# Routed feed-forward behind linear attention: which tables count which group, and which slots run after the last step

## The reference

```python
x = x + xattn(layernorm(x), ctx, ctx, ...)   # x, ctx: 128 x 128 x 256, float32
# xattn: q, k, v = linear; elu(q) + 1, elu(k) + 1; 16 heads of 16
#   sums over t of k_t v_t^T, read with q_t (causal), divided by the running sum of q; then @ Wo + bo
x = x + ffn(layernorm(x), W1, b1, W2, b2, expert_W, expert_b)
# ffn: h = relu(z @ W1 + b1); sel = argmax(h @ W2 + b2) over 8 experts
#   out = z @ expert_W[sel] + expert_b[sel], one expert for each token
```

## Time and profile before

| | us |
|---|---|
| median of three runs (range) | 1251.42 (1249.2 to 1252.38) |
| span of the profiled execution, first to last instruction | 1101.6 |
| mean granted TensorE clock in it | 0.977 |
| median less span | 149.8 |

### The profile page before, as it was taken

How to read it: one execution, slowest core, us unless ns; L and a number is a source line. 1 busy time by engine, 2 the same in 40 slices (tenths; PEclk the granted TensorE clock), 3 DMA queues, 4 the chain that set the end, 5 groups by cost and what they waited for, 6 DMA issues and landing times.

```text
span 1101.6 us, 37703 instructions
## 1 busy us (share of the span) xinstructions
PE 1010.6 (92%) x15724; PEld 723.6 (66%) x15724; DVE 879.8 (80%) x1908; ACT 374.5 (34%) x581; POOL 672.5 (61%) x578
## 2 busy tenths in 40 slices
PE   1869999999999999999999999999999999997683
PEld 1446666666777776776677777776676767776472
DVE  2468888998988988888988888888998888885552
ACT  0323333333333343343333333344333333331220
POOL 5134556555666666677666666677766566565755
PEclk9979999999999999999999999999999999998887
DMA  4743434444455445555555544445555544351451
GB/s 139 232 113 101 125 121 125 126 128 145 130 163 160 137 121 145 153 150 164 137 153 163 158 120 126 152 150 163 144 148 165 151 120 128 102 151 41 160 174 53
DMA packets 90920, 152.52 MB, mean 138 GB/s; under 512 B 19325, under 2 KB 57856, under 8 KB 90624
## 3 DMA queue, kind: packets, MB, share of 16 engines
q1 hardware_dynamic: 68864, 107.82, 35.3%
q0 software_dynamic: 12672, 33.84, 8.4%
q10 hardware_dynamic: 9216, 8.46, 3.7%
HBM read 98.20 MB, written 36.13 MB: 122 GB/s over the span
## 4 chain that ended last, share of the span: by engine, by line
PE 78%; DVE 8%; issue 4%; DMA 2%; SPq 1%; POOL 0%; ACT 0%; DVEq 0%; POOLq 0%; ACTq 0%
PE b_a L916 23%; PE b_b L921 18%; PE b_s L1006 9%; PE b_b L953 6%; PE b_s L930 6%; PE b_b L963 5%; DVE stage L634 3%; PE b_s L943 3%; PE b_s L971 2%; PE b_a L911 2%; PE b_s L991 2%; DVE kp L783 1%; DVE st L769 1%; DVE vsel L790 1%; DMA out<-rows 1%
## 5 line engine op out<-in xcount | busy, mean ns | idle before, releaser
L634 DVE TENSOR_TENSOR stage<-b_s,causal 128x1024 f32<-128x1024 f32 x192 | 225.5, 1215 | 6.7 <-PE b_s L930 4.2
L466 POOL DMA_INDIRECT out<-rows x136 | 160.3, 1178 | 45.1 <-issue 34.6
L458 POOL DMA_INDIRECT buckets<-row,place x128 | 141.6, 1106 | 34.5 <-issue 34.2
L916 PE MATMUL b_a<-x_T,wq_sb 128*128 128x512 f32 x256 | 128.9, 628 | 18.7 <-POOL x_T L483 14.2
L475 POOL TENSOR_TENSOR onehots<-onehots,onehot 128x32 bf16<-128x32 bf16 x32 | 7.8, 243 | 193.7 <-DVE place L754 193.7
L921 PE MATMUL b_b<-wo_sb,attT 128*128 128x256 f32 x512 | 121.3, 391 | 2.9 <-DVE attT L831 2.9
L916 PE MATMUL b_a<-ctxT,wk_sb 128*128 128x512 f32 x256 | 118.4, 605 | 1.8 <-ACT pos L530 1.8
L921 PE MATMUL b_b<-wv_sb,ctxT 128*128 128x256 f32 x512 | 119.0, 386 | 0.0
L483 POOL TENSOR_TENSOR x_T<-x_T,scale 128x1024 f32<-128x1024 f32 x32 | 75.5, 2360 | 65.6 <-DMA scale<-scales 64.8
L1006 PE MATMUL b_s<-we_sb,x3T 128*128 x464 | 113.2, 389 | 1.0 <-ACT x3T L539 1.0
L497 POOL TENSOR_TENSOR x_res<-x_res,bias_o 128x1024 f32<-128x1024 f32 x32 | 105.8, 3305 | 5.7 <-DMA x_res<-in_x 5.5
(11 more groups left out here) (125 smaller groups left out, 1794.2 us busy)
## 6 DMA issues: line engine op xcount, KB each, us to landing
rows<-buckets SPq DMA_DIRECT2D x136, 130.0 KB
x_in<-in_x SPq DMA_DIRECT2D x32, 512.0 KB, 4.1
x_T<-in_xT SPq DMA_DIRECT2D x32, 512.0 KB, 4.0
ctxT<-in_ctx SPq DMA_DIRECT2D x32, 512.0 KB, 4.6
qsel<-qp SPq DMA_DIRECT2D x256, 64.0 KB, 2.4
x_res<-in_x SPq DMA_DIRECT2D x32, 512.0 KB
scale<-scales ACTq DMA_DIRECT2D x32, 256.0 KB, 3.9
out<-rows POOLq DMA_INDIRECT x136, 3.4
```

What stands on the lines that cost most here:

```text
L458: pool.indirect_dma_start(buckets, bass.IndirectOffsetOnAxis(place[:, slot(route), t:t + 1], 0), row[:, slot(route), t, :], None).then_inc ...
L466: pool.indirect_dma_start(out.rearrange("t p n -> (t p) n"), bass.IndirectOffsetOnAxis(rows2[:, r, TOKEN:TOKEN + 1].bitcast(U32), 0), rows ...
L634: dve.tensor_tensor(dst.rearrange("p g h s q -> p g (h s) q"), b_s[:, :, 256 * t:256 * t + 256].rearrange("p g (a q) -> p g a q", q=C), ca ...
L916: last = pe.matmul(dst, w[:, k, P * h:P * h + P], rows[:, k, :], start=(k == 0), stop=(k == KC - 1))
```

## The change

- A table is filled in steps 8, 10, ..., 34 (eight slots each), one of four slots in step 35, and the last, now of 20 slots, in step 36. The ranks of the step before a table count the group that is being merged too (four more small products), so the table of step j counts the group routed in step j. SyncE's loads therefore wait for the scatter of that group, which is the one of the step before the loads.
- Quads run in steps 9 to 36. Step 34's quad is an extra one: its turn and products stand between the scores on TensorE, its biases before the second masks on VectorE, its sums after the last masks. Step 35 has two quads: the extra one as before, and one whose turn stands behind that of `x2n` and whose products stand around the logits. The tail has five quads, slots 116 to 135.
- In step 35 GpSimd scatters one tile of the routed group before `scale2` and three after it; before, all four came at the step's end. Extra quads are scattered to `out` in their own step.
- The 20 last slots have their own rows (`tail_rows`, in the memory of the attention's `stage`) and own semaphores, without a wait for the ring. They wait for the attention to be through with `stage`.
- The pads are issued on a signal of their own (`s_pad_at`), ahead of the last table's.
- In the tail no row is loaded ahead of the wait for the buckets.

```diff
-    TABLE_STEPS = range(9, STEPS - 1, 2)
+    TABLE_STEPS = list(range(8, STEPS - 2, 2)) + [STEPS - 2]
+    TABLE_SIZES = [BATCH] * (TABLES - 1) + [QUAD]
+    EARLY = sum(TABLE_SIZES)
+    LAST = SLOTS - EARLY
...
+        tail_rows = stage[:, 0:LAST * ROW].rearrange("p (r n) -> p r n", n=ROW)
...
-        quad_of = quads(TABLE_STEPS[0] + 1, STEPS - 1 - TABLE_STEPS[0], 0)
-        extra_of = {STEPS - 2: quad_of.pop(STEPS - 2)}
-        EARLY = quad_of[STEPS - 1][-1] + 1
+        quad_of = quads(TABLE_STEPS[0] + 1, STEPS - 2 - TABLE_STEPS[0], 0)
+        extra_of = {STEPS - 3: quad_of.pop(STEPS - 3), STEPS - 2: quad_of.pop(STEPS - 2)}
+        quad_of[STEPS - 2] = range(EARLY - 2 * QUAD, EARLY - QUAD)
+        quad_of[STEPS - 1] = range(EARLY - QUAD, EARLY)
...
+        def rows_of(i):
+            return rows2[:, i % RING, :] if i < EARLY else tail_rows[:, i - EARLY, :]
+
+        def rows_in(i):
+            return (s_rows2[i % RING], 16 * (i // RING) + 16) if i < EARLY else (s_tail_rows[i - EARLY], 16)
...
-                    routed = TABLE_STEPS[table] - STAGES
+                    routed = TABLE_STEPS[table] - STAGES + 1
                     sp.wait_ge(s_bucket[routed % 2], 16 * GT * (routed // 2 + 1))
                     sp.wait_ge(s_bucket[1 - routed % 2], 16 * GT * ((routed + 1) // 2))
                     sp.wait_ge(s_tab, TAB * table + TAB)
...
-                    if i >= RING:
-                        sp.wait_ge(s_outs[r], 16 * (i // RING))
+                    if RING <= i < EARLY:
+                        sp.wait_ge(s_outs[i % RING], 16 * (i // RING))
...
-            for quad in TAIL[:1]:
-                load_slots(quad)
             sp.wait_ge(s_spare, 16)
-            sp.wait_ge(s_tab, TAB * TABLES + TAB)
+            sp.wait_ge(s_pad_at, 1)
...
             for e in range(E):
                 sp.dma_start(buckets[bass.ds(pads[e], P), :], pad_row[:, :]).then_inc(s_pad, 16)
+            sp.wait_ge(s_tab, TAB * TABLES + TAB)
+            load_table(mybir.EngineType.SP, TABLES, first_rows)
+            sp.wait_ge(s_o, NG)
             for s in range(2):
                 sp.wait_ge(s_bucket[s], 16 * GT * (NG // 2))
             sp.wait_ge(s_pad, 16 * E)
-            load_table(mybir.EngineType.SP, TABLES, first_rows)
-            for quad in TAIL[1:]:
+            for quad in TAIL:
                 load_slots(quad)
...
+                    if j == STEPS - 2:
+                        scatter_rows(route, range(1))
...
                 if merge and j == STEPS - 2:
                     scale2(merge)
+                    scatter_rows(route, range(1, GT))
...
+                if merge and not attend:
+                    turn_out(slots_of(j))
...
-                turn_out(slots_of(j))
+                if attend or not merge:
+                    turn_out(slots_of(j))
...
+                if attend and extra_slots_of(j):
+                    pe.wait_ge(s_x1, n(merge, 2, 2))
+                    turn(extra_slots_of(j))
                 if attend:
...
                     late_scores(attend, 2, 1).then_inc(s_sb, 1)
+                    multiply(extra_slots_of(j)[0:2])
...
                     early_scores(attend, 1).then_inc(s_sc, 1)
-                if extra_slots_of(j):
+                    multiply(extra_slots_of(j)[2:4])
+                if extra_slots_of(j) and not attend:
...
                     turned(b_a, x2n).then_inc(s_x2Tp, 1)
+                if merge and not attend and slots_of(j):
+                    pe.wait_ge(s_mc, 2 * NG)
+                    turn(slots_of(j))
...
                     logit_products().then_inc(s_lg, 1)
+                if merge and not attend:
+                    multiply(slots_of(j)[2:4])
...
-                    ranks(group_no(merge) == NG - 1).then_inc(s_rank, 1)
+                    ranks(j + 1 in TABLE_STEPS or j + 1 == STEPS - 1).then_inc(s_rank, 1)
```

More of the change, by code:

```diff
@@ L221, in build @@
         s_outs = [sem(f"s_outs{r}") for r in range(RING)]
+        s_tail_rows = [sem(f"s_tail_rows{r}") for r in range(LAST)]
+        s_tail_outs = sem("s_tail_outs")
+        s_pad_at = sem("s_pad_at")
         s_x3Tp = sem("s_x3Tp")
@@ L341, in load_slots @@
             def load_slots(slots):
[L342 removed]
+                if slots and opens_table(slots[0]) and slots[0] < EARLY:
                     table = table_of(slots[0])
[L344 removed]
+                    routed = TABLE_STEPS[table] - STAGES + 1
                     sp.wait_ge(s_bucket[routed % 2], 16 * GT * (routed // 2 + 1))
@@ L454, in scale2, with scatter_rows @@
                                  tokens[:, bass.ds(n(merge, GT), GT)]).then_inc(s_token, 1)
-            def scatter_rows(route):
-                for t in range(GT):
+            def scatter_rows(route, tiles=range(GT)):
+                for t in tiles:
                     pool.indirect_dma_start(
@@ L487, in step @@
                     scale2(merge)
-                if not attend:
-                    for quad in (extra_slots_of(j - 1), slots_of(j - 1)):
-                        scatter(quad)
+                if not attend and j < STEPS - 1:
+                    scatter(extra_slots_of(j))
+                if not attend and j == STEPS - 1:
+                    scatter(slots_of(j - 1))
                 if attend:
@@ L499, in step @@
                                        ALU.add).then_inc(s_xb, 1)
-                if route and j < STEPS - 1:
+                if route and j < STEPS - 2:
                     scatter_rows(route)
+                if attend:
+                    scatter(extra_slots_of(j))
                 if load:
@@ L664, in whole_blocks @@
                 if up:
-                    dve.tensor_tensor(pad_of[:, :], counts, pad_at[:, :], ALU.add)
+                    dve.tensor_tensor(pad_of[:, :], counts, pad_at[:, :], ALU.add).then_inc(s_pad_at, 1)
                 return done
             def fill_table(table, up):
-                first = BATCH * table
-                slots = LAST if up else BATCH
+                first = first_of(table)
+                slots = size_of(table)
                 before_it = TAB * table
@@ L1009, in multiply, with ranks @@
                         last.then_inc(s_prod, 1)
-            def ranks(last_group):
+            def ranks(count_group):
                 out_of = b_a[:, 1, 0:GT * E]
@@ L1110, in step @@
                     expert_means(j - 5)
-                if slots_of(j):
+                if slots_of(j) and (attend or not merge):
                     if not attend:
```

55 lines of the change are left out of this document (29 added, 26 removed).

## The result

| | median us | range, executions |
|---|---|---|
| kernel before | 1250.47 | 1249.2 to 1252.38, 4 |
| changed kernel | 1258.21 | 1256.87 to 1259.4, 4 |

A forecast was written before the change was run, and what follows sets the result against it. TensorE was taken to bound the steps with quads, GpSimd's scatters the tail. Terms -10.4 - 2.4 + 1.4 + 3.4 + 1.3 = -6.7 us gave 1244.7 us from a median of 1251.42; range 1239.5 to 1251.8.

The forecast's parts named there:

- C: Tail's start: eight rows instead of four must land before the first product, 2.2 us lost.
- E: The quad added in step 9: 3.4 us lost, bounds 3.0 to 4.8.
- B: From the last place to the first late row load: pads issued earlier shorten 13.13 us to 8.5, 4.6 us gained.
- F: Counts in the loop: four more small products in the ranks of 14 steps, 1.3 us lost.
- A: Tail: eight scatters fewer at GpSimd's pace of 1.30 us each, 10.4 us gained.
- D, step 34: The quad's turn and products move into TensorE's waits for the masks, 2.0 us gained.
- D, step 35: First quad waits for just-scattered rows and a second quad is added; with step 34's gain, 1.4 us lost in all.
- G: Steps 9 to 33: row loads wait for the step before's scatter, covered by 9.7 us, price 0.
- R5: Rival: row loads, not GpSimd, pace the tail, so the sum comes near 0, 1251 us; chance 0.04.
- R3: Rival: new waits for late landings eat the tail's gain, -1.7 us in all, 1249.7 us; chance 0.16.
- R4: Rival: the loop's new wait makes 13 table-opening quads late; 1 us each gives +6.3 us, 1257.7; chance 0.06.
- signs of being wrong: Loop waits for row loads, gaps among the tail's 20 scatters, or a step 35 much over 16 us.

The follow-up runs named there:

- r0: The kernel before, unchanged, profiled a second time, in the 1250 kind of session: 1247.36 us with a span of 1245.6 us.
- e5: The changed kernel, unchanged, in the 1105 kind of session: 1110.07 us against 1104.61 for the kernel before, ratio 1.0041.
- e2: The kernel before with only the counts changed, so row loads wait for the step before's scatter; 1105 kind: 1104.61 us, ratio 0.9993.
- r1: The changed kernel, unchanged, profiled again in the 1250 kind of session: 1256.38 us.
- e16: The kernel before with own rows for the last 20 slots, pads on their own signal, step 34's quad between the scores; 1250 kind: 1245.3 us against 1249.1.
- e15: The changed kernel with only step 34's quad back in its old place; 1250 kind: 1255.1 us against 1249.1 for the kernel before.
- e3: The changed kernel without the quad of step 9, tail of 24 slots; 1105 kind: 1103.48 us against 1104.83 for the kernel before, ratio 0.9978.
- e6: The changed kernel without step 9's quad and with step 34's in its old place; 1105 kind: 1104.84 us against 1104.61 for the kernel before, ratio 1.0008.
- e9: The same kernel as e16, in the 1105 kind of session: 1102.92 us against 1107.60 for the kernel before, ratio 0.9958.
- e1: The kernel before with only own rows for the last 20 slots and pads on their own signal; 1105 kind: 1101.99 us against 1104.83, ratio 0.9966.
- e14: The kernel before without the scatters to `out` of slots 0 to 95; 1250 kind: 1175.6 us against 1254.22.
- e7: The same kernel as e14, in the 1105 kind of session: 1099.94 us against 1105.32 for the kernel before, ratio 0.9951.

## Why the prediction was wrong

**The step that failed** is the one in the sum: "The median of 1251.42 lies 149.8 us above the span; I leave that part as it is." It was inside the steps. Every price of the loop and of step 34 was then read at the wrong rate: a steady step lasts 36.2 us in r0, 30.9 in the rows. Second, in the kind that the rows did show, C, step 35 and E were too small by 2.9, 2.65 and 2.3 us and the gain of B too large by 1.1. That takes the whole gain away: outside steps 11 to 33 the e5 column adds up to +0.4. The rest of e5's loss lies in steps 11 to 33, where the forecast had 1.3 for F, and stays unexplained. Term by term, us (the tail's split counts from the last ranks; loss positive):

| term | forecast | e5 less before | changed less r0 |
|---|---|---|---|
| A, tail scatters | -10.4 | -10.4 | -12.8 |
| B, to the first late load | -4.6 | -3.5 | -8.4 |
| C, to the first scatter | +2.2 | +5.1 | +10.5 |
| D, step 34 | -2.0 | -2.5 | +4.6 |
| D, step 35 | +3.35 | +6.0 | +2.35 |
| E, steps 8, 9, 10 | +3.4 | +5.7 | +9.3 |
| F, counts | +1.3 | nothing that shows (e2) | not measured alone |
| G, new wait in the loop | 0 | nothing that shows (e2) | not measured alone |
| 11-32 and 33 | 0 | +6.4 | +5.6 (r1: +3.2) |

(D was forecast at +1.35 in all, 2.0 of gain in step 34 included. The last row holds the odd steps as well. The profiled pair differs by 11.2 us and the medians by 7.7, since r0 is a low execution of its kernel.)

**A** was right, by its own reason: 28 scatters in 36.43 us became 20 in 26.00, 1.30 each. In the timed kind they take 1.48 each before and 1.43 after, with gaps of up to 3.1 and 2.1 us. R5 falls for the 1105 kind.

**B** was right in kind. From the last place to the first late load it is 9.1 us in e5 (forecast 8 to 9) in place of 13.1, and 10.5 in place of 17.7 in the timed kind. But what comes last is still the pads: in e5 the landing of the last one, 3.31 us from 1054.87, and in the timed kind SyncE's own issues. Chain of the changed kernel, pads (L422) and row loads (L377):

```profile
1192.65 0.69 SPq L422
...
1202.71 0.71 SPq L377
...
1207.05 0.33 SPq L377
...
1208.08 3.13 DMA stage<-buckets
...
1213.80 6.60 PE b_b L1035 x16
```

**C** was too small. Its sum has one term for TensorE's side, four rows more; in e5, where the loads do follow at 0.54 us, another stands beside it:

```profile
1068.22 5.82 PE L1035 MATMUL b_b<-we_sb,x3T 128*128 x16 [1.81 <-issue]
```

From the first late load to these products it is 9.8 us, 5.0 before (1051.02). The turn of the eighth row ends 8.0 us after that load, where the fourth ended at 5.2: 2.8 us for the four rows more, forecast 2.2. Then TensorE reads the last table, five reads (L311) from 1065.7 to 1068.0, and stands idle for 1.81 us; before, its six reads of the table lay beside the sixteen products. The slow products are no news: 5.82 us, and 5.22 before. In the timed kind SyncE adds to it. Its first late loads are 2.1 to 2.8 us apart while GpSimd issues scatters to `out`, and from 1207.05 on, 1.9 us after the last of these, they are 0.52 apart, so the eighth load stands 8.7 us behind the first, 3.7 in e5. The chain above has both paces. The products take 6.60 us there (granted clock 0.56 over them; 3.72 warm), 4.30 in r0. The Trainium skill's fit, page "DMA: Bandwidth & Descriptors", section on the anatomy of one DMA, is of DMAs that GpSimd issues. So the estimate of 2.3 us that the prediction works out from it bears on the bucket scatters, whose landing no run here times alone; the late row loads are SyncE's, with a median of 2.8 us on the changed kernel's page and 3.13 in the chain.

**D, step 34** was right where TensorE is as fast as in the profile that I read, and wrong in sign where it isn't. Timeline of the changed kernel's step 34, which begins at 1131.47:

```profile
1141.16 3.54 PE L973 MATMUL b_s<-qsel,kp 32*64 32x128 f32 x64 [2.28 <-DVE stage L666]
1144.63 3.63 PE L1035 MATMUL b_b<-we_sb,x3T 128*128 x8
1147.42 2.35 DVE L666 TENSOR_TENSOR stage<-b_s,causal 128x1024 f32<-128x1024 f32 x2 [6.40 <-remote]
...
1151.48 2.52 PE L983 MATMUL b_b<-stage,vsel 128*32 128x64 f32 x72 [2.35 <-DVE rows L750]
1154.16 0.41 PE L983 MATMUL b_b<-stage,vsel 128*32 128x64 f32 x2 [0.15 <-issue]
...
1158.75 0.97 POOL L489 DMA_INDIRECT out<-rows  x1 [0.30 <-issue]
...
1161.71 3.63 PE L946 MATMUL b_a<-x2T,w_sb 128*128 128x512 f32 x4
```

The second pair of products takes 3.63 us in place of 2.00 (the granted clock is 0.54 over it and 0.74 over the step; 0.93 in e5). That isn't the change's doing alone: in r0's step 34 (0.81) the first pair takes 3.54. VectorE's masks begin 2.7 us behind the early scores, as the first four scatters to `out` end (1146.57). Then the late sums meet eight scatters in a row: the four to `buckets` and the quad's own four, which the change puts into the same step (the last at 1158.75 to 1159.72). They go in bursts from 1154.16 until 1161.71, 10.2 us in all. In e5 they take 1.99, and the early sums 1.94 in the midst of such scatters. That the quad is the cause is shown by e16 (+5.0 us with it) and e15 (-6.6 without it); the split between clock and bursts was not measured.

**D, step 35** had the right mechanism and order of waits, and even the right time for the rows: in e5 the turn of the fourth row begins 30.7 us behind step 34's ranks, where the forecast has it landed at 30.9 (1019.8 less 988.94). What failed is the price of the products behind that wait, 3.72 us warm: they take 6.23 (granted clock 0.59 over them), 2.5 of the 2.65 us that were missing. R3 had +4 for D, but from late landings, which didn't come. The length of 20.1 us was one of the signs of being wrong.

**E** was too small in both kinds. I had no row for the new table in step 8. It lies in VectorE's way there: in e5 TensorE waits 1.70 us for attT late in that step, and before it doesn't wait. In the 1105 kind step 8 lasts 28.0 to 28.3 us without it and 29.8 to 31.9 with it, e3 and e6 included, where step 9 has no quad. In the timed kind it lasts 29.1 to 30.3 without and 30.0 to 30.5 with it, so there it isn't told from chance. Step 9 itself costs 4.2 in e5 and 3.3 in the timed kind, where step 10 adds 4.7 for the scatters and their late signals: a quad in a steady step there is 36.04 - 29.44 = 6.6 us, and one in the tail 5.7 to 5.9. In that kind, moving one up loses by itself.

**R4** was the forecast for slower and isn't what happened: with the loop's wait alone (e2) the time is the same, and in the changed kernel's profiles of both kinds TensorE never waits for rows in steps 9 to 33.

What stays open: what makes a session of the one kind or the other, why scatters hold back other engines' signals and SyncE's issues in one and not in the other, why some signals beside them are in time, the odd steps of 32 to 34 us, and what makes steps 11 to 33 longer with quads from step 9 in the 1105 kind.

## What to carry to other kernels

Hold the span of a profile against the time of the same execution before pricing anything from it: where they differ by a tenth, the rows belong to other conditions, and terms worked out from them can have the wrong sign. Work moved from a tail into a loop is worth only the difference of its price in both places, so price the whole unit there, with its scatters and its table, in the first steps as well as in the steady ones. A quad put into one step's idle time won 2.5 us there in e5 and 0.6 in e9, but the next step then waited for rows in e5, and in e16 the same quad cost 5.0; own rows and the pads' own signal paid in both kinds (e1, e9, e16). Work put behind a wait for rows is priced at the lower clock level, and with the table reads that stand between the wait and the work.

## What was unexpected of the hardware

- One program took 1104 to 1108 us in some sessions and 1247 to 1254 us in others, at nearly the same mean granted clock (0.977 and 0.953).
- In the longer kind, beside GpSimd's indirect scatters, ACT's copy of x2T came 2.4 to 3.2 us behind TensorE's turn in each of 24 steps (0.04 in the other kind, and 0.04 in step 35 in both), VectorE read the logits once 7.8 us late, and TensorE's small products came in bursts every 0.76 us. Four scatters to `out` cost a step 3.3 us (e14), against 0.2 in the other kind (5.4 us over 24 quads, e7).
- In it SyncE's DMA issues take 0.70 us in place of 0.33 to 0.35, nearly the period of the bursts, while GpSimd issues scatters and for 1.8 to 1.9 us after the last one ends (in r0 until 1186.25, in the changed kernel until 1206.95). Then they are back at 0.33 to 0.35.
- Sixteen products right behind a wait for rows took 4.3 to 6.6 us in place of 3.72, at granted clocks down to 0.56.
